# A fused cross-attention and mixture-of-experts kernel: router products cut into four pieces among the query matmuls, and the maxima transposed one step earlier

## The reference

```python
def xattn(x, context):                       # d = 512, 16 heads of 32
    q, k, v = x @ Wq.T + bq, context @ Wk.T + bk, context @ Wv.T + bv
    attn = softmax(einsum('bhtd,bhcd->bhtc', q, k) / sqrt(32))
    return einsum('bhtc,bhcd->bhtd', attn, v) @ Wo.T + bo
def ffn(x):                                  # 8 experts, top 2
    w = softmax(x @ W_router.T + b_router)
    w = w kept at its two largest, zero elsewhere
    return einsum('bseo,bse->bso', einsum('bsd,eod->bseo', x, W_experts) + b_experts, w)
x = x + xattn(layernorm(x), ctx)
x = x + ffn(layernorm(x))
```

## Time and profile before

| | |
|---|---|
| median of 3 runs | 1334.58 us |
| lowest and highest | 1327.47 and 1335.1 us |
| span of the profiled execution | 1340.9 us |
| PE busy | 1224.7 us, 91% |
| DVE, POOL, ACT busy | 66%, 56%, 54% |

### The profile page before, as it was taken

The page is one execution under the profiler, slowest core; times in us unless marked ns, Lnnn a source line. Parts: engine busy times, 40 slices in busy tenths (PEclk is TensorE's granted clock), DMA queues, the critical chain, the costliest instruction groups (busy, mean ns, idle before and its releaser), DMA issues. The chain is left out here.

```text
span 1340.9 us, 36001 instructions
## 1 busy us (share of the span) xinstructions
PE 1224.7 (91%) x11024; PEld 735.1 (55%) x11025; DVE 881.3 (66%) x1933; ACT 722.1 (54%) x1040; POOL 744.6 (56%) x980
## 2 busy tenths in 40 slices
PE   8887999998999989999999986869899999999997
PEld 4445665655655655665655654534354555555454
DVE  4657787877868867867877867545445555555454
ACT  4336875775775775775766662624333333334333
POOL 4003555675675675675675674864644445444545
PEclk9879999999989998989989997889999999999999
DMA  8842664584583574583583573967999989998886
GB/s 267 253 135 65 173 176 153 148 254 142 150 258 130 142 241 152 147 262 131 144 237 115 132 215 109 357 221 156 199 177 184 175 173 188 179 172 155 168 165 133
DMA packets 135547, 239.22 MB, mean 178 GB/s; under 512 B 18440, under 2 KB 49416, under 8 KB 134280
## 3 DMA queue, kind: packets, MB, share of 16 engines
q1 hardware_dynamic: 102391, 161.24, 41.2%
q0 software_dynamic: 29808, 67.73, 25.2%
q10 hardware_dynamic: 3232, 8.68, 1.9%
HBM read 112.00 MB, written 101.40 MB: 159 GB/s over the span
## 5 line engine op out<-in xcount | busy, mean ns | idle before, releaser
L1854 PE MATMUL S<-we_s,wq_s 128*128 x1620 | 376.3, 382 | 12.6 <-DVE att L1832 5.8
L1782 POOL DMA_INDIRECT out<-xn,to x135 | 208.9, 1547 | 212.7 <-DMA out<-xn,to 123.6
L1854 PEld LDWEIGHTS S<-we_s,wq_s 128*128 128x128 f16 x1620 | 158.1, 98 | 180.8 <-issue 22.3
L1172 POOL TENSOR_TENSOR we_s<-P_s,we_s 128x1024 f16<-128x1024 f32 x96 | 204.2, 2136 | 65.6 <-ACT we_s L927 65.3
L1793 ACT ACTIVATE wq_s<-PVp 128x512 f16<-128x512 f32 x137 | 81.6, 597 | 272.4 <-PE PVp L1844 247.1
L1252 POOL DMA_INDIRECT dispatched<-xn,idx x128 | 131.7, 1029 | 92.6 <-ACT xn L620 52.1
L975 DVE TENSOR_REDUCE mx_sb<-S 128x6 f32<-128x924 f32 x160 | 171.3, 1111 | 11.3 <-PE S L726 9.1
L708 PE MATMUL W<-we_s,wq_s 128*128 128x512 f16 x512 | 168.7, 409 | 8.7 <-ACT mT L933 5.3
L746 PE MATMUL W<-wo_s,aT_hi 128*128 128x512 f16 x512 | 164.5, 383 | 2.6 <-DVE aT_lo L953 1.4
L1832 DVE SCALAR_TENSOR_TENSOR att<-S,be_s 128x512 f32<-128x512 f32 x135 | 93.3, 691 | 111.0 <-PE S L1854 101.5
L1810 DVE TENSOR_TENSOR wq_s<-PVp,wq_s 128x512 f16<-128x512 f32 x137 | 94.6, 691 | 38.3 <-ACT wq_s L1793 35.1
(11 more groups left out here) (207 smaller groups left out, 2039.8 us busy)
## 6 DMA issues: line engine op xcount, KB each, us to landing
P_s<-dispatched SPq DMA_DIRECT2D x139, 260.5 KB
we_s<-we_s SPq DMA_DIRECT2D x186, 128.0 KB, 6.0
be_s<-in_x SPq DMA_DIRECT2D x16, 1024.0 KB, 9.1
xR_s<-in_x SPq DMA_DIRECT2D x16, 1024.0 KB
out<-xR_s SPq DMA_DIRECT2D x16, 1024.0 KB
wst<-in_weT SPq DMA_DIRECT2D x16, 512.0 KB, 6.2
we_scratch<-wsp SPq DMA_DIRECT2D x16, 512.0 KB, 5.5
Kst<-k_scratch SPq DMA_DIRECT2D x16, 480.0 KB, 5.1
```

The lines of the kernel that those rows point to most:

```text
L1172: e.tensor_tensor(Pst[1][:, r:r + 2, :], exps(n), Pst[0][:, r:r + 2, :], ALU.subtract).then_inc(pldp, 1)
L1782: e.indirect_dma_start(out, bass.IndirectOffsetOnAxis(ap=to[u][:, :], axis=0), yw[u % YW], None, bounds_check=N - 1, oob_is_err=False, com ...
L1854: m = e.matmul(Yp[:, u % 2, :], gT[u % 2][xp][:, k, :], we_s[:, bass.ds(n * WN + (wp * KC + k) * D, D)], start=(c == 0), stop=(c == 11))
```

## The change

MT is issued ahead of PV5 instead of behind it. LA and LB are no longer steps of their own: `pe_logits(..., j, s)` does, for token tile j of 4, eight matmuls of LA and nine of LB, and one such piece stands ahead of each of Q6, Q7 and Q8 and a fourth behind Q8. LA thereby works on block `bp2`, at the end of a slot, where it worked on the same block in the middle of the slot after. Q8 moves from the head of the next slot to the end of this one, so that the queries end ahead of ST0. LA's result lies behind LB's in bank 0 (`LACOL`) and not in bank 1. On DVE, `dve_RB` is split: the reduction stays, then comes `dve_RA`, then the sum of the logits as `dve_RL`. The bank of LB counts as empty after the reduction (`lbs`). The number of matmuls and their sizes stay.

```diff
-    def pe_LA(e, b, s):
+    LACOL = NJ * 2 * NE
+
+    def pe_LA(e, b, j):
         bank = BANK["LA"]
...
+        o = W[:, bank, LACOL + j * 2 * NE:LACOL + (j + 1) * 2 * NE]
...
+    def pe_logits(e, lb, la, j, s):
+
+        if j == 0:
+            if free := emptied("LB" if lb else "LA", s):
+                e.wait_ge(*free)
+        if la:
+            pe_LA(e, la, j)
+        if lb:
+            pe_LB(e, lb, j)
...
     def pe_slot(e, s):
...
-        if on_bp1:
-            pe_Q(e, bp1, 8, s)
...
-        if on_bp1:
-            pe_LA(e, bp1, s)
...
+        if on_bp1:
+            pe_MT(e, bp1, s)
         if on_b:
             pe_PV(e, b, 5)
-        if on_bp1:
-            pe_MT(e, bp1, s)
-        if on_bm1 and not bm1.last:
-            pe_LB(e, bm1, s)
-        if on_bp2:
-            pe_Q(e, bp2, 6, s)
-            pe_Q(e, bp2, 7, s)
+        lb = bm1 if on_bm1 and not bm1.last else None
+        la = bp2 if on_bp2 else None
+        for n in range(NJ):
+            if lb or la:
+                pe_logits(e, lb, la, n, s)
+            if on_bp2 and n < NJ - 1:
+                pe_Q(e, bp2, 6 + n, s)
...
     def dve_slot(e, s):
...
             dve_RB(e, bm3)
+        if on_b:
+            dve_RA(e, b)
+        if on_bm3 and not bm3.last:
+            dve_RL(e, bm3)
...
-        if on_b:
-            dve_RA(e, b)
```

More of the change, by code:

```diff
@@ L639, in build @@
             ("Q9", 1), ("AT1", -1), ("AT3", -1), ("XT0", 2), ("R", -2), ("XT2", 2), ("O3", -1), ("Q3", 2),
-            ("O9", -1), ("LB", -1),),
+            ("O9", -1), ("LB", -1), ("LA", 2),),
         1: (
-            ("AT0", -1), ("LA", 1), ("AT2", -1), ("O0", -1), ("XT1", 2), ("XT3", 2), ("Q0", 2), ("O6", -1),
+            ("AT0", -1), ("AT2", -1), ("O0", -1), ("XT1", 2), ("XT3", 2), ("Q0", 2), ("O6", -1),
             ("MT", 1), ("Q6", 2),),
@@ L652, in build @@
     EMPTIED = {"XT": (t1e, 4), "AT": (ate, 4), "Q": (qle, 4), "O": (x1s, 4), "MT": (mte, 1), "R": (rev, 2),
-               "LA": (lae, 1), "LB": (lbe, 4), "MX": (mxr, 11), "ST": (exd, 10)}
+               "LA": (lae, 1), "LB": (lbs, 1), "MX": (mxr, 11), "ST": (exd, 10)}
     def emptied(step, s):
@@ L841, in pe_LB @@
-    def pe_LB(e, b, s):
-        bank = BANK["LB"]
[L843 to L855, removed]
+        if j == 0:
+            e.wait_ge(t1e, b.at(4, 4))
+            if b.first:
+                e.wait_ge(p_bk, 5)
@@ new lines, in pe_LA, with pe_LB @@
+        o = W[:, bank, LACOL + j * 2 * NE:LACOL + (j + 1) * 2 * NE]
+        for k in range(KC):
+            e.matmul(o.rearrange("p (l e) -> p l e", l=2), xnT[0][:, k, j * P:(j + 1) * P], wr_s[:, :, k, :], start=(k == 0), stop=False)
+        for k in range(KC):
+            m = e.matmul(o[:, 0:NE], xnT[1][:, k, j * P:(j + 1) * P], wr_s[:, 0, k, :], start=False, stop=(k == KC - 1))
+        if j == NJ - 1:
+            m.then_inc(lap, 1)
+    def pe_LB(e, b, j):
+        bank = BANK["LB"]
+        if j == 0:
+            e.wait_ge(ate, b.at(4, 4))
+            if b.first:
+                e.wait_ge(p_rx, 5)
+        o = W[:, bank, j * 2 * NE:(j + 1) * 2 * NE]
+        for k in range(KC):
+            e.matmul(o.rearrange("p (l e) -> p l e", l=2), aT[0][:, k, j * P:(j + 1) * P], wx_s[:, :, k, :], start=(k == 0), stop=False)
+        e.matmul(o[:, 0:NE], ones[:, :], cb_r[:, :], start=False, stop=False)
+        for k in range(KC):
+            m = e.matmul(o[:, 0:NE], aT[1][:, k, j * P:(j + 1) * P], wx_s[:, 0, k, :], start=False, stop=(k == KC - 1))
+        if j == NJ - 1:
+            m.then_inc(lbp, 1)
@@ L998, in dve_RA @@
             e.wait_ge(rcq, b.at(1, -1))
-        e.tensor_tensor(lga[p][:, :, :], W[:, BANK["LA"], 0:NJ * 2 * NE].rearrange("p (j e) -> p j e", e=2 * NE),
+        e.tensor_tensor(lga[p][:, :, :], W[:, BANK["LA"], LACOL:LACOL + NJ * 2 * NE].rearrange("p (j e) -> p j e", e=2 * NE),
                         st1[p][:, :].rearrange("p (j o) -> p j o", o=1).broadcast_to([P, NJ, 2 * NE]), ALU.mult).then_inc(lae, 1)
@@ L1006, in dve_RB, with dve_RL @@
         e.tensor_reduce(lgs[:, :, :], W[:, BANK["LB"], 0:NJ * 2 * NE].rearrange("p (j l e) -> p j e l", l=2, e=NE), AX, ALU.add).then_inc(lbs, 1)
+    def dve_RL(e, b):
         e.wait_ge(lbs, b.at(1, 1))
@@ L1993, in _ @@
             dve_RB(e, LAST)
+            dve_RL(e, LAST)
             dve_RM(e, LAST)
@@ L2030, in _ @@
             pe_tile(e, 0, 0)
-            pe_LB(e, LAST, LAST + (-(-1)))
+            for j in range(NJ):
+                pe_logits(e, LAST, None, j, LAST + (-(-1)))
             for u in range(1, TU):
```

## The result

The change made the kernel slower: 1347.46 us median of five runs (1344.05 to 1357.53) against 1334.58, ratio 1.011, 95% interval 1.007 to 1.015. The forecast was 1312.6 us. The profiled execution took 1355.8 us against 1340.9.

The account below looks back on a forecast made before the run. PE was taken as the bound. Per slot 0.30 - 0.82 + 0.03 - 1.2 = -1.7 us, -20 over twelve slots and -2 elsewhere, gave 1319 us profiled, 1312.6 us median; 8-in-10 range 1279 to 1331.

Parts of the forecast that it names:

- The bound and the mechanism: PE's own stream bounds the kernel; short matmuls stop beside POOL's scatters at a slot's end, 2.44 us more per slot.
- Neither continued nor reported as done: At a slot's end, a burst of short matmuls is held and its completion reported late, until 0.9 us after the last scatter.
- While scatters run: When the stop holds: throughout POOL's four scatters, 518.51 to 523.39 us in the slot shown, and about 0.9 us beyond.
- MT ahead: MT before PV5: +0.30 us per slot waiting for DVE's last maximum; Q6's `mT` wait, 3.5 us over eleven slots, goes.
- gain is eaten: Rival, chance 0.18: MT falls inside the scatters and is held too, `mT` stays late; -0.1 us per slot, 1331 us.
- The first stop: Behind piece 0, beside the first four scatters: 1.62 us instead of 2.44, so -0.82 us per slot.
- The pieces and LA: LA moved into the pieces at the slot's end: saves 0.80 us at AT2/AT3, costs 0.83, net +0.03 us per slot.
- Q8: Q8 ahead of the scores only moves four matmuls across a slot boundary: 0 us.
- The clock: Of 2.5 us per slot lost to half clock, 1.2 comes back; granted clock 0.96 to 0.97 over the eleven slots.
- The rival that ended on the slower side: Small matmuls among the queries keep the clock low: +3.1 us per slot, 1370 us, 1348 at half growth; chance 0.10.
- Right: Signs confirming the forecast: MT's 0.3 us wait, prompt `mT`, a gap behind piece 0, AT3's new wait, clock, 48.5 us slots.
- the first gap: Sign: an issue gap ahead of the first query matmul behind piece 0, ending 0.9 us after POOL's fourth scatter.

Follow-up runs that it names:

- e4: Kernel before with LB moved from behind MT to ahead of R in the middle of the slot, where no scatters run; ratio 1.011.
- e1: Kernel before with one edit, MT ahead of PV5; ratio 0.998.
- e5: Kernel before, unchanged, profiled on a chip that showed no holds; ratio 1.001, the kernel before taking 1281.1 us in that group.
- e2: Changed kernel with MT put back behind PV5; ratio 1.023, 1353.9 us.
- e8: Changed kernel with all eight of POOL's scatters together, behind the norm constants and RQ, on the chip of e5; ratio 1.068.
- e12: Changed kernel with LA back in one piece behind ST4 and its DVE step back too, LB still in four pieces; ratio 0.991.
- e3: Changed kernel with Q8 put back at the head of the next slot, behind piece 3; ratio 1.011.
- e14: Changed kernel with eight slots instead of four per turn of PE's loop, so it is never branched back; ratio 1.002.
- e6: Kernel before with MT ahead of PV5 and LB ahead of R in the middle of the slot, on the chip of e5; ratio 1.010.

## Why the prediction was wrong, step by step

*The bound and the mechanism.* PE's stream was the right thing to count. "Neither continued nor reported as done" named two effects, and both are there: in e4 PE loses 3.0 us per slot at Q6 to a report that is late by some 2.2, and in e1 it stops 1.2 us per slot among short matmuls though the profile shows nothing that it waits for. No run shows whether one makes the other. "While scatters run" was too wide: MT is still reported on time behind the start of the third (e4 above). That the hold needs scatters rests on their place in every slot; no run on a chip with holds moved them. And it is no fixed cost of this program (e5).

*MT ahead.* Priced +0.30, measured +0.19. Its return was put at the 3.5 us of `mT`; e2 shows that with the order of the change it saves 18.7 us of that wait. The rival "gain is eaten" fell: `mT` is on time.

*The first stop.* Forecast 1.62 us instead of 2.44, counted as the time by which the first query matmul is put off. Counted so, from MT's start, the kernel before has 3.74 us on average over the eleven slots and needs 1.37 undisturbed (176.68 - 175.31), which is 2.37 more. The change has 3.51 and needs 1.84 (0.44 + 0.95 + 0.45; in e8, the same order without holds, it is 1.82), which is 1.67 more. This step was right in place, end and size. The listed waits are another measure (16.9 us before, 13.3 after, over eleven slots) and leave out the matmuls that trickle through; the prediction's 15.7 leaves out L852's 1.2 as well.

*The pieces and LA.* This step failed. LA was costed where it stands, +0.03 us a slot, and its own rows are as forecast: AT3 waits 0.42 for the low part (forecast 0.45). What I left out is what it pushes: a second stop, 10.4 us over eleven slots or 0.95 a slot, was put at nothing without a reason. With LA's 0.83 us and Q8 ahead of it, piece 3 and PV6, 17 and 30 short matmuls with only ST0's and ST1's long ones between, stand beside the second four scatters, a group that only the count of 128 in the earlier trace rows, eight a slot, shows and that never entered the sum. In the kernel before it starts at 529.82 in the slot of the earlier trace rows and meets long products and PV6, without a gap. By e12 LA's place costs 27.0 / 11 = 2.5 us a slot on a chip with holds, against the 0.03 of the sum. Of the 27.0 us, 12.1 are listed waits, and PE's busy time is 516.12 - 502.08 = 14.0 us longer for the same matmuls. The clock, 0.96 instead of 0.97, is part of these 14.0; the rest is not broken down.

*Q8.* Put at 0; right (e3).

*The clock.* Forecast 0.97 and 1.2 us a slot; measured 0.96, some 0.5 us (27.6 us lost before, 0.04 x 563.8 = 22.6 after). As the clock is printed with two digits, 0 to 1 us would fit as well, and PE's busy time did not fall (516.50 before, 518.57 after). New stops came as the old shrank.

*The loop.* Not in the sum. The branch back lies between two slots: 2.2 us before, 5.7 in the change; with the restacked queries (3.8 us more) that is 7.3 us, and e14 takes 0.9% off. What sets the edge's price is open. It is not the step that stands there: in e3 that is Q8, as before, and the wait is 7.1. Nor is it the holds: in e8, the changed kernel on the chip of e5, it is 6.2.

*The waits together.* Listed waits grew by 43.9 - 35.2 = 8.7 us of the 12. Down went the first stop (3.6), `mT` (3.5) and the waits of AT transposes (11.6 to 5.4, so 6.2). Up went the second stop (10.4), the edge (3.5), the restacked queries (3.8), MT (2.1) and two small ones (2.2).

Sum over eleven slots: the forecast's -1.7 a slot became +1.1. The rival that ended on the slower side was right in sign alone: its cause, a longer low clock, did not come. Of the signs under "Right", those of MT, `mT`, the first gap, AT3 and the clock all came true, and the time was still wrong: none of them looked at the scores and PV6 behind the pieces. Only the last, slots that last 48.5 us, failed (51.3).

## What to carry to other kernels

Ask of each wait who is told late, not only who runs slowly: where semaphore increments can be held, put what another engine waits for ahead of the hold, and long products into it. A product that is moved must be followed to every later burst of transfers that it pushes the rest into. Compare orders only beside each other, on one chip and at one time, and look once at a chip on which the disturbance is missing: it shows about what it costs as a whole.

## What the runs showed of the hardware

Unexpected was the size of the difference between chips: the same program took 1281.1 us on one and 1322.5 to 1334.6 on the others. Of the 62.7 us between the two profiles, 44.6 lie in the eleven slots, as waits of TensorE and as busy time at a clock of 0.95 instead of 1.00. The fast chip was met in one group of runs only, and one chip gave 1324.4 and 1334.1 us within minutes; what makes either difference, the runs don't show.

On the chips with holds TensorE's increment for MT comes 1.8 to 2.2 us behind the fourth scatter's start, in each of the eleven slots of the kernel before and of e4, late by 2.2 to 2.5 us, if MT ends less than half a microsecond ahead of that start; if it ends 0.9 us ahead, it comes at once.

The branch back of a loop cost TensorE between 2.1 us (e6) and 7.1 us (e3, e12), once, with the same number of instructions in the turn but for a few. The Trainium skill ("Runtime: NRT & Kernel Launch", Instruction fetch mechanics) says that branching breaks the sequential prefetch. The traces agree that the edge costs, with these numbers; what sets the size within the range is open.
